# Rows normalised, split and scattered before the expert tiles, halves fetched by a transposing transfer, and a new order of each engine's work

## The chip, the cores and the metric

The kernel runs on one core of a Trainium2 chip. A core has a matrix engine (TensorE, "PE" in the profile, its weight loads "PEld"), VectorE ("DVE"), ScalarE ("ACT"), GpSimd ("POOL") and SyncE ("SP"), which mainly issues transfers. Each engine executes its own stream of instructions in order and waits on semaphores for the others. Sixteen DMA engines carry the transfers. The metric is the device time of one execution in microseconds (us). Three runs of the kernel before took 492.33, 501.55 and 499.98 us, median 499.98.

## The reference

The input `x` is 16 x 256 tokens of 256 features, so T = 4096 rows of D = 256. There are two layers with residuals.

```
x = x + xattn(layernorm(x), ctx, ctx)       # per token: 16 heads of 16 features attend to each other, causal over heads
x = x + ffn(layernorm(x), ...)              # mixture of E = 8 experts, one per token

# ffn:
logits = xf @ gate_w.T + gate_b;  top1 = argmax(logits)
for e in range(8):
    h = relu(xf @ w1[e].T + b1[e])          # 256 -> 1024
    y = h @ w2[e].T + b2[e]                 # 1024 -> 256
    out += where(top1 == e, y, 0)
```

Everything is fp32. To keep that precision the kernel splits fp32 operands into two fp16 halves (a high part and the rest) and adds the products that matter.

## The kernel before, in words

**The attention** goes in 16 steps of 256 tokens (`NC` = 16). A step has a score product of 96 small matmuls (line 1111), a softmax on DVE, ACT and POOL, four transposes of the weights on TensorE (line 1129), and an output product of 96 matmuls (line 1143). The stationary operands of both products are block diagonal. They are built in SBUF by transfers that "spread" a compact tile `qv_hl` into a zeroed part of `arena`: eight small transfers a step, five issued by SP and three by ACT (`spread_part`, line 305; 307 for the last two steps). Step i's spread carries the values of step i and the queries of step i+2, so it waits for output product i-1 and score product i, and output product i waits for it. The fp16 rests of keys, queries and values are made on POOL (lines 995, 987, 1003).

**The groups.** Four steps make a group of 1024 tokens (`NG` = 4). When its outputs are there, TensorE computes gate logits (line 1171) and turns the rows back to token order (line 1156); ACT copies them to `pay` (line 531), DVE takes mean and variance (lines 726 to 735), POOL takes the power -0.5 (line 1029), DVE writes -mean/std beside it (line 738). DVE picks the expert (`choose`) and TensorE ranks the tokens, and POOL scatters the rows of `pay` to `sorted_rows` in DRAM, sorted by expert, with eight indirect transfers (line 1050). A row of `pay` has ROW = 260 words: 256 of x, the shift, the scale, the token number and a zero. After the last group SP fills the gaps behind each expert's rows with twelve transfers (`fill`, line 433).

**The expert tiles.** 39 tiles of 128 sorted rows follow (`NTILES` = 39). Tiles 0 to 8 may start after the second group is scattered, tiles 9 to 16 after the third, tiles 17 to 38 after the fourth. For each tile SP reads its place from a list, fetches its rows (line 451, buffers `FR` = 6) and its expert's biases (lines 456 and 457). ACT normalises the rows (line 566, in `expert_inputs`), TensorE transposes them with two fp32 transposes (line 1196), ACT casts the high half out of PSUM (line 571) and DVE makes the low half (line 906). Then come `ups`, 8 blocks of 6 matmuls (line 1229), into two PSUM banks; DVE adds the bias (line 915), ACT takes the relu as high half (line 580), DVE the rest (line 926); `downs`, 8 blocks of 2 matmuls (lines 1245 and 1246); DVE adds the result to the row (line 940), to which POOL had added the second bias (line 1069), and POOL scatters it to the output (line 1076).

**The order of the work.** On each engine the work is written as several generators ("lanes"), each yielding a due time before each piece. `weave` (line 41) runs, piece by piece, the lane with the earliest due time, and so makes the engine's one stream. The due times are numbers written by hand or by a rule: `tile_at(j)` is 240 + 5.7 j, and blocks of `ups` and `downs` of neighbouring tiles alternate one by one. The due times set only the order: a piece waits in its engine's stream for its semaphores, and everything behind it waits too. The precision of the products, the buffers of hidden units (`h_in`, two halves) and the two PSUM banks of each product are the same for all tiles.

## Time and profile before

| | |
|---|---|
| runs | 492.33, 501.55, 499.98 us, median 499.98 |
| profiled execution | span 492.6 us from the first to the last instruction; no time outside the span is given for it |
| PE, DVE, POOL, ACT busy | 82%, 70%, 42%, 36% of the span |
| mean granted TensorE clock | 0.962 of full speed |
| costliest group | line 1229 on PE, 158.6 us |

The span is 0.3 us over the fastest of the three runs and 7.4 us under their median. The attention's first output product starts at 47.0 us and its last one ends at 238.3. The first expert block on PE starts at 241.1 and the last instruction ends at 492.6. A busy time on PE is the sum of durations of pipelined matmuls, so it must be read beside the starts of the instructions.

### The profile page before, as it was taken

Reading aid. Unit: us, or ns where it says so; the run is one execution under the profiler, and the core shown is the slowest. Engines: PE = TensorE matmul, PEld = TensorE weight load, DVE = VectorE, ACT = ScalarE, POOL = GpSimd, SP = SyncE. Lnnn points to the kernel's source line nnn. Section 1 sums busy time; section 2 is a strip of 40 time slices with the busy share of each in tenths; the row PEclk is TensorE's granted clock in tenths of the full one; section 3 lists DMA queues with packets and bytes.
Section 4 is the critical chain, followed back from the end, with each engine's and each line's share of the span. In section 5 each row is a group of like instructions: output and inputs, shape, how many; then the busy total and the mean of one; then the engine's idle time right before and its main releaser. Section 6 shows DMA issues by size and latency. Waiting matters only on the chain.

```text
span 492.6 us, 16316 instructions
## 1 busy us (share of the span) xinstructions
PE 402.1 (82%) x5967; PEld 338.3 (69%) x5967; DVE 346.3 (70%) x777; ACT 177.5 (36%) x317; POOL 208.7 (42%) x213
## 2 busy tenths in 40 slices
PE   0135868888888866897999999779999999999992
PEld 0025757887787765896887877557778877877871
DVE  7978969789945863477757877457666666766662
ACT  3343255542624221342434433224333333433420
POOL 8345374334673467523723242642333323233221
PEclk9999999999999999975699999889999999999998
DMA  8999578899685664377612232544333322222210
GB/s 282 414 305 218 135 170 241 212 259 260 160 220 119 152 167 107 106 173 181 207 45 67 68 76 81 185 131 155 90 68 77 77 62 62 69 60 61 84 31 0
DMA packets 105162, 69.39 MB, mean 141 GB/s; under 512 B 78077, under 2 KB 88190, under 8 KB 104576
## 3 DMA queue, kind: packets, MB, share of 16 engines
q1 hardware_dynamic: 75696, 56.67, 41.9%
q10 hardware_dynamic: 25984, 3.21, 4.6%
q0 software_dynamic: 3408, 8.46, 4.6%
q8 instruction: 53, 0.87, 0.7%
q14 instruction: 21, 0.17, 0.1%
HBM read 48.28 MB, written 12.57 MB: 124 GB/s over the span
## 4 chain that ended last, share of the span: by engine, by line
PE 55%; DMA 11%; SPq 9%; DVE 9%; issue 6%; POOL 5%; ACT 2%; ACTq 1%; another core or an unknown queue 1%; POOLq 0%; DVEq 0%
PE s_ps L1229 20%; SPq L305 8%; PE at_ps L1245 6%; DMA arena<-qv_hl 6%; PE pv_ps L1245 6%; PE pv_ps L1143 6%; PE s_ps L1111 3%; PE lg_ps L1171 3%; PE pv_ps L1246 3%; PE at_ps L1246 3%; POOL qv_hl L987 2%; PE tr_ps L1156 2%; DMA arena<-x 2%; PE st_ps L1196 2%; POOL k_hl L995 1%
## 5 line engine op out<-in xcount | busy, mean ns | idle before, releaser
L1229 PEld LDWEIGHTS s_ps<-arena 128*128 x1872 | 132.7, 99 | 52.2 <-issue 14.6
L1229 PE MATMUL s_ps<-arena 128*128 128x128 f16 x1872 | 158.6, 222 | 8.4 <-DVE arena L906 5.1
L915 DVE SCALAR_TENSOR_TENSOR arena<-arena,s_ps 128x512 f32<-128x512 f32 x78 | 53.6, 687 | 48.6 <-PE s_ps L1229 35.9
L1076 POOL DMA_INDIRECT result<-arena x39 | 38.8, 995 | 95.5 <-DVE arena L940 91.6
L1111 PEld LDWEIGHTS s_ps<-k_hl,arena 128*128 128x128 f16 x1536 | 54.3, 118 | 29.9 <-DMA arena<-qv_hl 22.1
L1111 PE MATMUL s_ps<-k_hl,arena 128*128 128x16 f16 x1536 | 54.7, 179 | 23.3 <-DMA arena<-qv_hl 19.3
L1143 PE MATMUL pv_ps<-a_hl,arena 128*128 128x16 f16 x1536 | 54.7, 179 | 19.7 <-DMA arena<-qv_hl 15.9
L1143 PEld LDWEIGHTS pv_ps<-a_hl,arena 128*128 128x128 f16 x1536 | 53.5, 118 | 22.8 <-DMA arena<-qv_hl 18.3
L1245 PE MATMUL at_ps<-arena,k_in 128*128 x160 | 60.9, 383 | 0.8 <-DVE k_hl L926 0.6
L1245 PE MATMUL pv_ps<-arena,x_in 128*128 x152 | 58.1, 383 | 0.1
L1069 POOL TENSOR_TENSOR arena<-arena 128x256 f32<-128x256 f32 x39 | 30.7, 786 | 60.7 <-DMA arena<-b 60.6
L580 ACT ACTIVATE k_in<-arena 128x512 f16<-128x512 f32 x40 | 25.2, 630 | 65.7 <-DVE arena L915 60.3
L580 ACT ACTIVATE x_in<-arena 128x512 f16<-128x512 f32 x38 | 23.9, 630 | 69.0 <-DVE arena L915 60.4
L898 DVE SCALAR_TENSOR_TENSOR arena<-arena 128x512 f16<-128x512 f32 x56 | 48.0, 926 | 0.8 <-ACT arena L558 0.7
L1246 PE MATMUL at_ps<-arena,k_hl 128*128 x160 | 43.8, 274 | 0.1
L1246 PE MATMUL pv_ps<-arena,x_in 128*128 x152 | 41.8, 275 | 0.0
L1050 POOL DMA_INDIRECT sorted_rows<-pay,slot_i x32 | 34.2, 1067 | 15.9 <-DVE slot_i L802 8.1
L558 ACT ACTIVATE arena<-arena 128x512 f16<-128x512 f32 x56 | 32.0, 621 | 17.4 <-DMA arena<-w 13.7
L926 DVE SCALAR_TENSOR_TENSOR k_hl<-arena,k_in 128x512 f16<-128x512 f32 x40 | 27.7, 693 | 11.0 <-ACT k_in L580 10.7
L1003 POOL TENSOR_TENSOR qv_hl<-v_in,qv_hl 128x512 f16<-128x512 f32 x16 | 21.6, 1353 | 30.6 <-ACT qv_hl L493 30.6
L926 DVE SCALAR_TENSOR_TENSOR x_in<-arena,x_in 128x512 f16<-128x512 f32 x38 | 26.9, 709 | 8.8 <-ACT x_in L580 8.5
L987 POOL TENSOR_TENSOR qv_hl<-x_in,qv_hl 128x512 f16<-128x512 f32 x16 | 22.1, 1384 | 20.7 <-ACT qv_hl L475 20.7
(143 smaller groups left out, 614.2 us busy)
## 6 DMA issues: line engine op xcount, KB each, us to landing
arena<-w SPq DMA_DIRECT2D x28, 512.0 KB, 6.1
arena<-sorted_rows SPq DMA_DIRECT2D x39, 130.0 KB, 2.4
arena<-b SPq DMA_DIRECT2D x39, 128.0 KB
arena<-qv_hl SPq DMA_DIRECT2D x70, 64.0 KB, 3.5
k_in<-k_t SPq DMA_DIRECT2D x16, 256.0 KB, 3.9
v_in<-v_t SPq DMA_DIRECT2D x16, 256.0 KB
arena<-x SPq DMA_DIRECT2D x4, 1024.0 KB, 12.1
o_sb<-x_r SPq DMA_DIRECT2D x16, 256.0 KB, 3.8
```

The source lines that it names most:

```text
L305: eng.dma_start(to, qv_hl[part, at].rearrange("p s b c u a -> p (s b) c u a")).then_inc(s_bd[i % 2], 16)
L580: eng.activation(h_hi[j % 2][:, c * HALF:(c + 1) * HALF], h_in[:, c], ACT.Relu).then_inc(s_h_hi, 1)
L898: eng.scalar_tensor_tensor(out=lo, in0=src, scalar=W_SCALE, in1=hi, op0=ALU.mult, op1=ALU.subtract).then_inc(s_w_lo, 1)
L915: eng.scalar_tensor_tensor(out=h_in[:, c].rearrange("p (k t) -> p k t", t=P), in0=bias, scalar=W_SCALE, in1=h_ps[c][:].rearrange("p (k t) ...
L926: eng.scalar_tensor_tensor(out=h_lo[j % 2][:, cols], in0=h_in[:, c], scalar=0.0, in1=h_hi[j % 2][:, cols], op0=ALU.max, op1=ALU.subtract). ...
L1050: eng.indirect_dma_start(out=sorted_rows, out_offset=bass.IndirectOffsetOnAxis(ap=slot_i[:, b:b + 1], axis=0), in_=pay[:, b, :], in_offset ...
L1076: eng.indirect_dma_start(out=out, out_offset=bass.IndirectOffsetOnAxis(ap=rows[:, r, :].bitcast(I32)[:, D + 2:D + 3], axis=0), in_=rows[:, ...
L1111: m = eng.matmul(s[:, n], q_bd[i % 2][:, n // 2, :, n % 2, q], k_hl[:, n, k, :], start=False, stop=(n, q) == (BLK - 1, 1))
L1143: m = eng.matmul(o[:, n], v_bd[i][:, n // 2, :, n % 2, v], a_hl[:, n, a, :], start=(n, a, v) == (0, 0, 0), stop=(n, v) == (BLK - 1, 1))
L1229: k = eng.matmul(o, weights_of(j, w + k_ * H + n * P, P), xt[:, j % 2, k_ * P:(k_ + 1) * P], start=k_ == 0 and w is HI_1 and xt is xt_hi, ...
L1245: eng.matmul(y[:], h_hi[j % 2][:, n * P:(n + 1) * P], weights_of(j, at, 2 * D), start=n == 0, stop=False)
L1246: k = eng.matmul(y[:, 0:D], h_lo[j % 2][:, n * P:(n + 1) * P], weights_of(j, at, D), start=False, stop=n == KH - 1)
```

## The change: what it does

1. **Rows are normalised per group.** A new lane `normalised_rows` on ACT computes, for each of 32 blocks of 128 rows, the normalised row into `xn1`, and casts it four blocks at a time to an fp16 high half `x1_hi`. A new lane `low_rows` on POOL subtracts it, four blocks at a time, for the low half `x1_lo`. Both halves stand in `pay` behind the old 260 words, so a row has ROW = 516 words, and the scatters (line 1050 before) and the fills carry the longer rows. The scatters wait for the low halves too.
2. **Tiles fetch the halves transposed.** For each tile SP issues a transposing transfer of 128 rows x 512 fp16 from DRAM into `xt` (three buffers, `XB`), besides the old 260 words into `rows`. Lane `expert_inputs` is gone from ACT, PE and DVE, and so is the PSUM use. The product of the first layer reads `xt` directly.
3. **Waits.** The transfer for tile j waits for `ups` of tile j-3. POOL's residual add waits for the rows themselves, not for ACT's normalising. DVE's bias add of a tile waits for the rest of the tile before it (`s_h_lo`).
4. **A new order.** The due times in the lanes are replaced by a table `TIMES` by engine and lane, which `weave` sorts. In it `ups` come 8 blocks together, in pairs of tiles with 2 blocks of `downs` between the two and 14 behind them. 21 blocks of `ups` (tiles 0, 1 and most of 2) stand ahead of the last output product on PE, and SP has the first fetches (rows of tiles 0, 1 and 2) ahead of the last spread. The first transfers of the program are in another order, and nearly all pieces of the attention change places.
5. `dynamic_dma_scratch_size` is 4096.

The core of the diff:

```diff
-def weave(*lanes):
-    due = [(next(lane, None), n) for n, lane in enumerate(lanes)]
...
+def weave(times, **lanes):
+    turns = sorted((t, n, k) for n, name in enumerate(lanes) for k, t in enumerate(times[name]))
+    lane = list(lanes.values())
+    for steps in lane:
+        next(steps)
+    for _, n, _ in turns:
+        next(lane[n], None)
...
-    ROW = D + 4
+    FETCHED = D + 4
+    ROW = FETCHED + D
+    sorted_halves = sorted_rows.bitcast(F16)
+        xn1 = sb("xn1", [P, G // 2, D])
+        x1_hi, x1_lo = [pay[:, :, FETCHED:].bitcast(F16)[:, :, n * D:(n + 1) * D] for n in range(2)]
-        FR = 6
+        FR, XB = 6, 3
-        TILE = 5.7
+        TILE = 5.3
...
 # SP, fetch
-                    eng.dma_start(rows[:, r, :], sorted_rows[bass.ds(row, P), :]).then_inc(s_rows[r], 16)
-                    yield tile_at(j) - 2.6
+                    if j >= XB:
+                        sp.wait_ge(s_up, 2 * (j - XB + 1))
+                    eng.dma_start_transpose(xt[:, j % XB], sorted_halves[bass.ds(row, P), 2 * FETCHED:]
+                                            ).then_inc(s_xt[j % XB], 16)
+                    eng.dma_start(rows[:, r, :], sorted_rows[bass.ds(row, P), 0:FETCHED]).then_inc(s_rows[r], 16)
+                    yield
...
 # ACT
-            def expert_inputs():
-                for j in range(NTILES):
...
+            def normalised_rows():
+                for g in range(NG):
+                    for m in range(2):
+                        half = slice(m * G // 2, (m + 1) * G // 2)
+                        for b in range(half.start, half.stop):
+                            yield
+                            act.wait_ge(s_ln1, g + 1)
+                            act.wait_ge(s_x1_lo, 2 * g + m)
+                            eng.activation(xn1[:, b - half.start], pay[:, b, 0:D], ACT.Identity, scale=pay[:, b, D + 1:D + 2],
+                                           bias=pay[:, b, D:D + 1]).then_inc(s_xn1, 1)
+                        yield
+                        act.wait_ge(s_xn1, G * g + half.stop)
+                        eng.copy(x1_hi[:, half], xn1[:]).then_inc(s_x1_hi, 1)
...
 # DVE
-            def expert_inputs():
...
 # hiddens
+                        dve.wait_ge(s_h_lo, 2 * (j - 1) + c + 1)
...
 # POOL
+            def low_rows():
+                for g in range(NG):
+                    for m in range(2):
+                        half = slice(m * G // 2, (m + 1) * G // 2)
+                        yield
+                        pool.wait_ge(s_x1_hi, 2 * g + m + 1)
+                        eng.tensor_tensor(x1_lo[:, half], xn1[:], x1_hi[:, half], ALU.subtract).then_inc(s_x1_lo, 1)
 # scatters
+                        pool.wait_ge(s_x1_lo, 2 * g + 2)
 # residuals
-                    pool.wait_ge(s_xn2, j + 1)
+                    pool.wait_ge(s_rows[j % FR], 16 * (j // FR + 1))
...
 # PE
-            def expert_inputs():
-                for j in range(NTILES):
-                    yield tile_at(j) + 0.6
...
-                            pe.wait_ge(s_xt_lo, j + 1)
-                            pe.wait_ge(s_xt_hi, j + 1)
+                            pe.wait_ge(s_xt[j % XB], 16 * (j // XB + 1))
...
-    nc = bacc.Bacc("TRN2", target_bir_lowering=False, num_devices=1)
+    nc = bacc.Bacc("TRN2", target_bir_lowering=False, num_devices=1, dynamic_dma_scratch_size=4096)
```

## Rows read from the trace of the kernel before

**Rows 1.** The page's span and its busy times of PE and DVE.

```profile
span 492.6 us, 16316 instructions
PE 402.1 (82%) x5967; PEld 338.3 (69%) x5967; DVE 346.3 (70%) x777; ACT 177.5 (36%) x317; POOL 208.7 (42%) x213
```

**Rows 2.** Busy time by stage; then mean granted clock, DMA share, GB/s.

```profile
47.00:235.00 188.00, 153.08 (x3063) 140.91 (x3064) 138.25 (x329) 73.77 (x128) 93.20 (x80) 0.95 0.71 178
216.00:243.30 27.30, 23.11 (x473) 21.38 (x471) 21.04 (x59) 10.43 (x18) 14.02 (x13) 0.50 0.67 196
241.00:300.00 59.00, 57.09 (x625) 47.10 (x624) 44.68 (x110) 23.26 (x45) 22.70 (x27) 0.98 0.28 75
300.00:350.00 50.00, 44.49 (x484) 34.44 (x483) 31.03 (x76) 14.97 (x28) 20.18 (x22) 0.93 0.44 140
350.00:478.00 128.00, 126.48 (x1477) 99.76 (x1476) 84.37 (x157) 46.55 (x89) 40.43 (x45) 1.00 0.27 67
```

**Rows 3.** Timeline of PE: starts of tiles 17 and 38, and a transpose pair.

```profile
355.23 0.62 PE L1229 MATMUL s_ps<-arena 128*128 128x128 f16 x6 [0.40 <-issue]
...
358.82 0.50 PE L1229 MATMUL s_ps<-arena 128*128 128x128 f16 x6
359.16 0.39 PE L1196 MATMUL st_ps<-ident,arena 128*128 128x128 f32 x2
359.38 0.38 PE L1245 MATMUL at_ps<-arena,k_in 128*128 x1
...
474.94 0.50 PE L1229 MATMUL s_ps<-arena 128*128 128x128 f16 x6
```

**Rows 4.** The transposes alone: duration in ns (min, median, max), first and last start.

```profile
L1196 PE MATMUL st_ps<-ident,arena x78: 272/278/456, 238.1 to 473.2; 128*128 128x128 f32 x78
```

**Rows 5.** The chain that ended last, within two attention steps: start, us, what.

```profile
110.94 3.39 PE pv_ps L1143 x96
...
114.46 0.60 SPq L305
...
118.19 3.47 DMA arena<-qv_hl
...
121.71 3.38 PE pv_ps L1143 x96
```

**Rows 6.** Timeline of PE: first and last output product, first expert block.

```profile
46.99 3.37 PE L1143 MATMUL pv_ps<-a_hl,arena 128*128 128x16 f16 x96 [2.23 <-DMA arena<-qv_hl]
...
237.83 0.45 PE L1143 MATMUL pv_ps<-a_hl,arena 128*128 128x16 f16 x9 [0.50 <-issue]
...
241.12 2.10 PE L1229 MATMUL s_ps<-arena 128*128 128x128 f16 x18
```

**Rows 7.** A stall at tile 11: ACT, PE; and DVE's group, 300 to 350.

```profile
312.82 0.37 ACT L571 CAST arena<-st_ps 128x256 f16<-128x256 f32 x1 [3.27 <-remote]
314.01 0.34 PE L1229 MATMUL s_ps<-arena 128*128 128x128 f16 x3 [2.66 <-DVE arena L906]
L906 DVE TENSOR_TENSOR arena<-st_ps,arena 128x256 f16<-128x256 f32 x7 | 2.9, 419 | 5.7 <-issue 3.0 <-ACT arena L571 2.8
```

**Rows 8.** Small-piece queue (packets, MB, share of 16 engines); the fetch's landing.

```profile
q10 hardware_dynamic: 25984, 3.21, 4.6%
arena<-sorted_rows SPq DMA_DIRECT2D x39, 130.0 KB, 2.4
```

**Rows 9.** Timeline of SP's queue: one tile's bias loads and the next fetch.

```profile
407.07 0.33 SPq L456 DMA_DIRECT2D arena<-b  x1
407.59 0.33 SPq L457 DMA_DIRECT2D arena<-b  x1
409.00 0.24 SPq L451 DMA_DIRECT2D arena<-sorted_rows  x1
```

**Rows 10.** Groups: ACT normalising (300 to 350), POOL rests and scatters (40 to 235).

```profile
L566 ACT ACTIVATE arena<-arena 128x256 f32<-128x256 f32 x7 | 4.1, 592 | 2.0 <-issue 1.4 <-DMA arena<-sorted_rows 0.6
L995 POOL TENSOR_TENSOR k_hl<-k_in,k_hl 128x512 f16<-128x512 f32 x14 | 17.0, 1215 | 26.4 <-ACT k_hl L484 26.4
L1050 POOL DMA_INDIRECT sorted_rows<-pay,slot_i x16 | 16.4, 1024 | 7.2 <-issue 3.6 <-DVE slot_i L802 3.5
```

More of the change, by code:

```diff
@@ L38, in wait_ge @@
             self.passed[sem] = value
-def weave(*lanes):
-    due = [(next(lane, None), n) for n, lane in enumerate(lanes)]
-    due = [d for d in due if d[0] is not None]
-    while due:
-        turn = min(due)
-        due.remove(turn)
-        again = next(lanes[turn[1]], None)
-        if again is not None:
-            due.append((again, turn[1]))
+def weave(times, **lanes):
[5 more added lines that the diff above has]
+        next(lane[n], None)
+    assert all(next(steps, True) for steps in lane)
 def xattn_moe_kernel(nc, x, x_t, x_r, k_t, v_t, gate_w, gate_b, w1, b1, w2, b2, out):
@@ L210, in xattn_moe_kernel @@
         s_rows = [sem(f"s_rows{n}") for n in range(FR)]
+        s_xt = [sem(f"s_xt{n}") for n in range(XB)]
         s_b1, s_b2 = [[sem(f"{w}_{n}") for n in range(2)] for w in ("s_b1", "s_b2")]
@@ L425, in fill @@
                     for m in range(1 if n < E - 1 else 1 + SPARE // (2 * P)):
-                        yield fill_at(next(at))
+                        yield
                         if n + m == 0:
```

423 lines of the change are left out of this document (236 added, 187 removed), and 98 rows, old and new, of tables (TIMES, act, op1).

## The prediction, as it was put on record before the changed kernel was run

> **What bounds the kernel now.** I read the page first: PE is busy 402.1 of 492.6 us, more than any other engine [rows 1]. Then the busy times by stage [rows 2], which show two kernels in one. In the attention, from 47 to 235 us, PE is busy 153.1 of 188 us and no engine fills the stretch. From 350 to 478 us PE is busy 126.5 of 128 us and DVE 84.4: there the matrix engine is the bound. Between them, from 300 to 350, PE is busy 44.5 of 50. Then the chain that ended last. In the attention it runs round a loop: output product, five issues on SP's queue, the landing of the spread, output product again. One turn is 121.71 - 110.94 = 10.8 us [rows 5]. From the first output product to the end of the last there are 237.83 + 0.45 - 46.99 = 191.3 us [rows 6]; fifteen turns of 10.8 and one product of 3.4 would be 165. So about 26 us of the attention are neither PE work nor the loop, but pieces that stood behind others in an engine's stream. In the expert stage tile 17 starts at 355.23 and tile 38 at 474.94 [rows 3], which is 119.7 / 21 = 5.70 us a tile.
>
> **The change part by part.** The sum is made against the profiled execution, whose span is 492.6 us. That is 0.3 over the fastest run and 7.4 under the median of 499.98.
>
> *a. The transposes leave PE.* There are 78, two a tile, with a median duration of 278 ns [rows 4]. Multiplied out that is 21.7 us, and it is the wrong reading, because durations on PE overlap. The pair starts at 359.16 and the next matmul at 359.38 [rows 3]: the pair costs PE 0.22 us. So 39 x 0.22 = 8.6 us go, and the pitch falls from 5.70 to 5.48 us. The Trainium skill ("TensorE: Matmul & The Clock Gate", Part 4: PE-mode transpose) gives about 275 ns for one in a kernel's context and says that access latency is most of it; the duration here agrees, and a sum made with it would be 78 x 0.275 = 21.5 us by that page, where the starts in the trace show a pair at 0.22. The other instructions that go (two on ACT and one on DVE a tile) free engines that have time to spare in that stage [rows 2]; I cost them at nothing, and PE is their cover.
>
> *b. New work in the groups.* ACT gets 32 normalisings at 0.59 us [rows 10] and 8 casts of 1024 columns. POOL gets 8 subtractions of 1024 columns, twice the 512 of line 995 at 1.2 us [rows 10], so 2.4 us each. In the attention ACT is busy 73.8 and POOL 93.2 of 188 us [rows 2]. Three groups bring POOL 6 x 2.4 = 14 us. POOL makes the rests of queries and values that a spread waits for, so a subtraction in front of one delays a turn of the loop. This can cost from 0 to 14 us; it is taken within the next term. The longer scatters and fills carry about twice the bytes. The DMA share is 0.44 where the fills are [rows 2], and in the new order all fills stand before the fetch of tile 11, so tile 17 does not wait for them: nothing.
>
> *c. The new order in the attention.* It can give back at most the 26 us above. It can give nothing, or cost, say, one more turn, 11 us, since each engine is in order and a piece that is late holds all behind it. I take half of the most, 13 us gained, because group work (gates, turned rows, rests) has to go somewhere in each four steps and PE has 35 idle us there, not more.
>
> *d. Expert work ahead of the last output product.* Before, the first expert block starts at 241.12, 2.8 us after the last output product [rows 6]. Now 21 blocks of 6 matmuls stand ahead of it. A block takes 0.34 us (358.82 to 359.16, rows 3), so 21 x 0.34 = 7 us go into PE's idle time. Bounds 0 to 7, I take 7.
>
> *e. The stalls near the fourth group.* Tile 11 starts after 2.66 us of idle PE, released by line 906, which had waited for line 571, which had waited 3.27 us [rows 7]; these two lines no longer exist. PE's idle time from 300 to 350 is 5.5 us, and two stretches at half clock of 3.4 us follow the stalls. I take 5 us gained, between 0 (another wait takes their place) and 10. What is late next: in SP's stream tile 10's fetch is between the fills, which wait for the fourth group's count, so a late routing would starve PE there.
>
> *f. SP's queue.* Per tile it takes 409.00 + 0.24 - 407.07 = 2.2 us of 5.70 [rows 9], and one issue more is 0.24 to 0.9 us (line 305's issues, rows 5, are 0.6 and up). Steadily this is hidden. But three fetches now stand ahead of the last spread, which the last output product waits for. That can cost 1 to 7 us; I take 2.
>
> *g. The clock.* From 216 to 243 the granted clock was 0.50, that is 1.2 GHz in place of 2.4, and it came when little wide work was there to be slowed [rows 2]. With expert blocks in that stretch such a spell would cost up to 13 us (half of 27). I take 2, since it may not come at all.
>
> The transposing transfer itself has no row. It moves 128 KB a tile. From below, the plain fetch of 130 KB lands in 2.4 us [rows 8]. From above, as pieces of 32 bytes: the queue of small pieces took 4.6% of 16 x 492.6 us for 25984 packets, 14 ns each [rows 8], and 4096 pieces over 16 engines are 3.6 us, or 7.2 if reading and writing do not overlap. I take 3.6 us plus 2.4 for landing, 6 us. The window from the end of `ups` j-3 to `ups` j is two tiles, about 11 us. So it is hidden and costs nothing. The Trainium skill ("VectorE: DVE Perf Modes", The three transpose paths) gives 1309 ns for a 128 x 128 two-byte transpose by DMA; four of them would be 5.2 us a tile, an estimate by that page, just inside the pitch, so the sum by it would not change but the margin is thin.
>
> Sum: 492.6 - 8.6 - 13 - 7 - 5 + 2 + 2 = 463.0 us. The runs before lie from 0.3 under to 9 over their profile, so I add 4, about half of the 7.4 to the median: **467 us**.
>
> **The rivals.**
>
> *Attention unmoved.* The new order brings new late pieces for old ones (c is 0) and the early blocks stand waiting in PE's stream (d is 0). Left are a, e, f: 492.6 - 8.6 - 5 + 2 = 481, with 4 added 485. For it: PE's and DVE's streams are already dense, and POOL has 14 us more. Against it: 26 us are there to be had.
>
> *Everything given back.* Also e stays, and the late routing at tile 10 costs what the transposes gave: about 495. This is also the case in which the change does not do what it says.
>
> *The transposing transfer is the bound (slower).* Its place is the fetch of every tile from tile 3 on. If the pieces are read and written one after the other, 7.2 us a transfer, and one transfer goes at a time, the pitch is 7.2 in place of 5.48: 36 x 1.7 = 62 us on top of 467, so 529 us. It decides from 5.48 us a transfer, or from a landing later than 11 us; at 6.3 us the gain is used up. For it: the pieces on the SBUF side are short, and such a stream has no row. Against it: DMA share is 0.27 in that stage [rows 2].
>
> **How the numbers follow.** Forecast 0.66, with a range of its own from 452 to 484 (c from 24 to 0, g up to 10). Attention unmoved 0.15 (478 to 494). Given back 0.06. The transfer as the bound 0.13. The range from 450 to 500 leaves out the last and a little below. A measurement of this kernel tells about 2% from no change, here 490 to 510. Faster by over 2%: 0.66 + 0.11 of the second case, 0.77. Within 2%: 0.04 + 0.06 = 0.10. Slower 0.13.
>
> **What the profile after would show.** a: no line like 1196, and tiles 5.4 to 5.5 us apart near the end; if they are 5.2, the pair was worth its duration. b: POOL subtractions near 2.4 us. c: the last output product ends near 225 to 230 us. d: expert blocks before it. e: no idle PE of about 3 us between tiles 10 and 14. f: landing of the transposing transfer well under 11 us. The prediction is wrong if `ups` of late tiles wait for `xt`, or if the output products still come 12.5 us apart on the mean.

## The result, and the profile of the changed kernel

The changed kernel took 530.42 us (median of 4 runs, 529.35 to 532.71) beside 500.69 us for the kernel before (492.33 to 501.55): the ratio is 1.074, with a 95% interval from 1.067 to 1.080. It is slower by 7.4%, where 467 us, with a range from 450 to 500, had been forecast: the prediction was wrong.

The page, in answer to [rows 1]. Columns as there.

```profile
span 529.3 us, 16204 instructions
PE 422.1 (80%) x5889; PEld 348.7 (66%) x5889; DVE 341.3 (64%) x738; ACT 165.1 (31%) x279; POOL 231.7 (44%) x221
```

TensorE has 5889 matmuls in place of 5967: exactly the 78 transposes are gone. Yet it is busy 20 us more. So the busy times of the matmuls that were there before must be longer, by clock or by their order; the stages tell which.

The stages, in answer to [rows 2], and the stretch at half clock: window, length, busy time of PE, PEld, DVE, ACT, POOL, granted clock, DMA share, GB/s.

```profile
47.00:235.00 188.00, 141.02 (x2789) 130.86 (x2790) 137.16 (x265) 82.93 (x143) 97.61 (x82) 0.84 0.71 179
235.00:300.00 65.00, 55.06 (x737) 47.74 (x735) 41.35 (x109) 20.11 (x35) 27.26 (x27) 0.79 0.56 142
300.00:350.00 50.00, 43.43 (x398) 29.96 (x397) 32.25 (x83) 14.20 (x24) 26.05 (x23) 0.93 0.88 242
350.00:478.00 128.00, 125.32 (x1321) 97.11 (x1319) 66.90 (x122) 25.49 (x42) 39.49 (x41) 1.00 0.38 81
173.80:259.20 85.40, 62.74 (x1212) 58.46 (x1213) 60.52 (x152) 36.25 (x62) 43.85 (x37) 0.50 0.67 164
```

Two things stand out. From 47 to 235 us TensorE issues 2789 matmuls, not 3063: the attention is behind. From 350 to 478 us it is busy 125.3 of 128 us at full clock, as before, but with 1321 matmuls in place of 1477. The transposes of some 23 tiles are 46 of the 156 missing; the rest are matmuls that follow each other more slowly.

TensorE's timeline, in answer to [rows 3, 6]: first output product (L1313), first expert block (L1386), last output product, first of the fourth group's turned outputs (L1325), starts of tiles 18 and 38.

```profile
53.13 3.34 PE L1313 MATMUL pv_ps<-a_hl,arena 128*128 128x16 f16 x96 [6.24 <-DVE a_hl L886]
...
253.38 8.28 PE L1386 MATMUL s_ps<-arena 128*128 128x128 f16 x96 [3.68 <-issue]
...
264.53 3.34 PE L1313 MATMUL pv_ps<-a_hl,arena 128*128 128x16 f16 x96
...
273.38 0.69 PE L1325 MATMUL tr_ps<-ident,o_sb 128*128 128x128 f32 x4
...
389.54 3.58 PE L1386 MATMUL s_ps<-arena 128*128 128x128 f16 x48
393.02 0.38 PE L1402 MATMUL at_ps<-arena,k_in 128*128 x1
...
514.44 1.70 PE L1386 MATMUL s_ps<-arena 128*128 128x128 f16 x24
```

From the starts the 36.7 us of span divide into stages. They are read in the same way in every kernel below: the end of the last output product, the start of tile 17, the start of tile 38.

| | last product ends | tile 17 | tile 38 | span |
|---|---|---|---|---|
| before | 238.3 | 355.2 | 474.9 | 492.6 |
| changed | 267.9 | 381.1 | 514.4 | 529.3 |
| longer by stage | +29.6 | -3.7 | +13.6 | -2.8 |

The attention loses 29.6 us and the steady expert stage 13.6 (about 2 us of this come back in the last column: tiles now go in pairs, and tile 17 is the second of its pair, tile 38 the first of its own). The steady pitch is (514.44 - 389.54) / 20 = 6.2 us, where 5.48 was forecast. The row of tile 18 says where: its 48 up matmuls (L1386) stand in a row and take 393.02 - 389.54 = 3.48 us, 72 ns each. In the kernel before 6 of them take 0.34 us [rows 3], 57 ns each.

VectorE's timeline, in two places that TensorE waited for:

```profile
45.06 7.32 DVE L1069 SCALAR_TENSOR_TENSOR arena<-arena 128x512 f16<-128x512 f32 x6
52.31 0.68 DVE L886 TENSOR_TENSOR a_hl<-at_ps,a_hl 128x512 f16<-128x512 f32 x1
...
114.44 0.69 DVE L868 TENSOR_REDUCE rowmax<-s_ps 128x32 f32<-128x512 f32 x1 [2.28 <-PE s_ps L1283]
...
117.84 2.38 DVE L903 BATCH_NORM_STATS2 bn<-pay 128x6 f32<-128x256 f32 x7
120.14 0.62 DVE L907 BATCH_NORM_AGGREGATE bn<-bn 128x2 f32<-128x6 f32 x8
...
123.26 0.69 DVE L875 TENSOR_TENSOR a_sb<-s_ps,rowmax 128x512 f32<-128x512 f32 x1
```

Six low halves of expert weights (7.3 us) stand ahead of the first softmax result. Later a whole group's layer norm stands between the row maximum (L868) at 114.44 and the subtraction (L875) at 123.26.

SP's queue ahead of the last output product: the third fetch (a transposing transfer), then the last spread.

```profile
254.79 1.22 SPq L646 DMA_TRANSPOSE arena<-sorted_rows  x1
256.21 0.41 SPq L648 DMA_DIRECT2D arena<-sorted_rows  x1
256.68 3.78 SPq L506 DMA_DIRECT2D arena<-qv_hl  x5
```

### The profile page after: what moved, and what is told of

The parts are those of the page before. It is cut to its first block, busy times and chain, and to the rows that moved or that the text cites. A ratio compares the mean times of both kernels' runs of the same rounds, so it can differ in the third digit from the quotient of the medians.

```text
span 529.3 us, 16204 instructions
## 1 busy us (share of the span) xinstructions
PE 422.1 (80%) x5889; PEld 348.7 (66%) x5889; DVE 341.3 (64%) x738; ACT 165.1 (31%) x279; POOL 231.7 (44%) x221
## 4 chain that ended last, share of the span: by engine, by line
PE 66%; DVE 20%; issue 6%; POOL 3%; DMA 2%; SPq 1%; ACT 1%; POOLq 0%; DVEq 0%; ACTq 0%
PE s_ps L1386 26%; PE at_ps L1402 7%; PE pv_ps L1402 6%; PE pv_ps L1313 6%; PE lg_ps L1339 5%; PE s_ps L1283 5%; DVE arena L1069 4%; PE at_ps L1403 3%; PE pv_ps L1403 3%; PE tr_ps L1325 2%; DVE bn L903 2%; PE at_ps L1300 2%; DVE xbn L823 1%; DMA arena<-x 1%; POOL xstat L1146 1%
## 5 line engine op out<-in xcount | busy, mean ns | idle before, releaser
L1386 PE MATMUL s_ps<-arena 128*128 128x128 f16 x1872 | 144.2, 220 | 10.4 <-issue 8.7
L1386 PEld LDWEIGHTS s_ps<-arena 128*128 x1872 | 127.9, 98 | 30.2 <-issue 15.0
L1246 POOL DMA_INDIRECT result<-arena x39 | 46.3, 1187 | 79.9 <-DVE arena L1105 71.6
L1313 PE MATMUL pv_ps<-a_hl,arena 128*128 128x16 f16 x1536 | 54.6, 180 | 30.1 <-DVE a_hl L886 20.6
L1313 PEld LDWEIGHTS pv_ps<-a_hl,arena 128*128 128x128 f16 x1536 | 54.0, 118 | 33.9 <-issue 19.7
L769 ACT ACTIVATE k_in<-arena 128x512 f16<-128x512 f32 x40 | 23.3, 623 | 156.5 <-PE at_ps L1403 135.7
L1105 DVE SCALAR_TENSOR_TENSOR arena<-at_ps,arena 128x256 f32<-128x256 f32 x40 | 17.0, 424 | 79.0 <-PE at_ps L1403 78.4
L1402 PE MATMUL at_ps<-arena,k_in 128*128 x160 | 56.9, 390 | 2.1 <-DVE k_hl L1091 1.7
L1402 PE MATMUL pv_ps<-arena,x_in 128*128 x152 | 51.5, 384 | 1.9 <-DVE x_in L1091 1.9
L1403 PE MATMUL pv_ps<-arena,x_in 128*128 x152 | 41.9, 275 | 0.0
L1175 POOL TENSOR_TENSOR a_sb<-a_sb,inverse 128x512 f32<-128x512 f32 x16 | 18.4, 1150 | 34.8 <-DVE inverse L883 34.8
L1300 PE MATMUL at_ps<-ident,a_sb 128*128 128x128 f32 x64 | 17.7, 429 | 16.4 <-POOL a_sb L1175 16.0
L1339 PEld LDWEIGHTS lg_ps<-gate_bd,o_sb 128*128 128x128 f32 x128 | 28.8, 312 | 2.0 <-issue 1.6
```

The lines of the kernel that those rows point to most:

```text
L769: eng.activation(h_hi[j % 2][:, c * HALF:(c + 1) * HALF], h_in[:, c], ACT.Relu).then_inc(s_h_hi, 1)
L1246: eng.indirect_dma_start(out=out, out_offset=bass.IndirectOffsetOnAxis(ap=rows[:, r, :].bitcast(I32)[:, D + 2:D + 3], axis=0), in_=rows[:, ...
L1313: m = eng.matmul(o[:, n], v_bd[i][:, n // 2, :, n % 2, v], a_hl[:, n, a, :], start=(n, a, v) == (0, 0, 0), stop=(n, v) == (BLK - 1, 1))
L1339: m = eng.matmul(LG, o_sb[:, :, h], gate_bd[:, h].rearrange("p b e -> p (b e)"), start=h == 0, stop=h == HEADS - 1)
L1386: k = eng.matmul(o, weights_of(j, w + k_ * H + n * P, P), xt[:, j % XB, a + k_], start=(k_, w, a) == (0, HI_1, 0), stop=k_ == KD - 1 and w ...
L1402: eng.matmul(y[:], h_hi[j % 2][:, n * P:(n + 1) * P], weights_of(j, at, 2 * D), start=n == 0, stop=False)
```

## The experiments

Chips differ, for the kernel before most of all: 476 to 487 us on three of them, 492 to 505 on the others. So each ratio is to the kernel before on the same chip, and stages are compared by their starts. "Old order" is that of the kernel before, "new order" that of the changed kernel; an order is edited by renumbering the tables of positions. Every kernel with the changed data path also has its smaller parts (VectorE's wait for the rests of the tile before, the scratch size of 4096); no run separates these.

**The yardstick: the changed kernel again.**

> The changed kernel, unaltered, on the same chip as the others of this call, as the yardstick for them. Expected: last output product ends near 268 us, pitch 6.2 us, 1.06 to 1.08 times the kernel before.

Measured: 523.60 us, ratio 1.086 [1.079, 1.094]; last product ends at 265.6, tile 17 at 372.7, tile 38 at 506.3, span 521.1. As expected. Its clock was 0.997 on the mean in place of 0.909. Of the 8.2 us between the two spans, 2.3 lie in the attention (267.9 - 265.6) and 6.1 between there and tile 17, after the long stretch at half clock had ended at 259.2. The clock is not shown to be the cause. The four runs of the first result took 529.35, 529.84, 531.01 and 532.71 us with mean granted clocks of 0.854, 0.910, 0.909 and 0.983, so the shortest had the lowest clock; of the four runs here the shortest had the highest (522.88 us with 0.997, 524.80 with 0.865). Neither way is it more than 3.4 us. The other difference between the two is the chip.

**The changed data path in the old order (e1).** The new pieces are slotted in behind their group's mean and variance:

```diff
 # positions on GpSimd, shortened
-scatters of a group: 8 pieces, one by one between the attention's
+low_rows 0, low_rows 1 of the group, then its 8 scatters
 # on ScalarE: 10 normalised_rows behind the group's layer_norms
 # expert stage: up and down blocks alternate one by one, as before
```

> The changed data path (normalised rows as halves, transposing transfer, no transposes on TensorE) with every lane back in the order of the kernel before; the new pieces (normalising on ScalarE, subtraction on GpSimd) stand one group step behind their group's mean and variance. Theory 1, the new order is the cost and the data path a gain: last output product ends near 238 to 242, tile pitch 5.48 us (5.70 less the 0.22 of a pair of transposes), time about 480 to 487 us. Rival, the data path (transposing transfer, its time on SP's queue, longer rows) is the cost: pitch stays at 6.2 or the attention still ends near 268, time 515 to 530 us.

Measured: 503.46 us, ratio 1.048 [1.041, 1.056]; last product ends at 254.5, tiles 17 and 38 at 374.5 and 486.8, so 5.35 us a tile, span 500.9. On another chip 502.48 and 1.050. Both theories hit one half: the pitch is what the transposes should give, but the attention is 16.2 us longer than before (254.5 - 238.3) though its order is the old one. The longest of the waits is this, in TensorE's timeline:

```profile
211.21 1.11 PE L1242 MATMUL at_ps<-ident,a_sb 128*128 128x128 f32 x4 [9.96 <-POOL a_sb L1117]
```

and GpSimd's timeline ahead of it:

```profile
196.35 2.16 POOL L1142 TENSOR_TENSOR pay<-xn,pay 128x1024 f16<-128x1024 f32 x1
203.41 2.12 POOL L1142 TENSOR_TENSOR pay<-xn,pay 128x1024 f16<-128x1024 f32 x1 [4.90 <-ACT pay L702]
206.43 1.07 POOL L1162 DMA_INDIRECT sorted_rows<-pay,slot_i  x1 [0.90 <-POOL pay L1142]
207.81 0.98 POOL L1162 DMA_INDIRECT sorted_rows<-pay,slot_i  x1 [0.30 <-issue]
209.09 0.97 POOL L1162 DMA_INDIRECT sorted_rows<-pay,slot_i  x1 [0.30 <-issue]
210.08 1.07 POOL L1117 TENSOR_TENSOR a_sb<-a_sb,inverse 128x512 f32<-128x512 f32 x1
```

GpSimd is idle 4.90 us in front of the second subtraction, waiting for ScalarE's cast (L702), then issues three scatters, and only then scales the softmax weights (L1117) for which TensorE has been idle almost 10 us. The granted clock is no rival here: the kernel before ends its attention at 236.6 with a clock of 0.81 in it (its second profile, below), this kernel at 253.2 with 0.80 (its second profile, too).

**Alternating blocks in the new order (e2).**

```diff
 # TensorE from tile 17 on
-ups j (8 blocks in a row), downs (8 blocks in a row)
+ups j block 0, downs block, ups j block 1, downs block, ...
 # VectorE and GpSimd, same tiles: rests, results and stores in the order that this needs
```

> The changed kernel with its new order up to tile 16, and from tile 17 on the blocks of up and down products alternate again, one by one, as in the kernel before. Theory, 48 up matmuls in a row are slower than the same ones between down products: pitch falls from 6.2 to 5.48 us over 22 tiles, so 16 us less, time about 514 us; the attention stays as it is (last output product ends near 268). Rival, the pitch is set by the transposing transfer or by VectorE: pitch and time unchanged, 529 to 531 us.

Measured: 502.62 us, ratio 1.048 [1.040, 1.057]; last product ends at 266.8, tile 17 at 375.8, tile 38 at 486.7: (486.7 - 375.8) / 21 = 5.28 us a tile. Against the ratio 1.086 of the unaltered changed kernel this one edit gives back 0.038 of 482, 18 us. (The medians, on two chips with nearly the same kernel before, differ by 21.) Transfer, work and instructions are the same; only the order from tile 17 on differs.

**The same from the other side: the kernel before with blocks in a row (e3).**

```diff
-yield tile_at(j) + 2.6 + UNIT * n
+yield tile_at(j) + 2.6 + 0.01 * n
...
-yield tile_at(j) + 8.65 + UNIT * n
+yield tile_at(j) + 8.65 + 0.01 * n
```

> The kernel before, with its transposes on TensorE, where only the order of the expert stage is changed: the eight up blocks of a tile stand in a row, and the eight down blocks too. Theory as for the alternating kernel, from the other side: pitch rises from 5.70 to about 6.4 us, over 39 tiles 28 us more, time about 520 us. Rival, the order of blocks costs nothing: pitch 5.70, time 493 to 500 us.

Measured: 576.59 us, ratio 1.198 [1.188, 1.207]; pitch 8.22 us. The direction holds, the size was far under. Its timeline on TensorE, tile after tile:

```profile
393.05 3.88 PE L1229 MATMUL s_ps<-arena 128*128 128x128 f16 x48 [1.23 <-DVE arena L906]
401.14 3.97 PE L1229 MATMUL s_ps<-arena 128*128 128x128 f16 x48 [1.23 <-DVE arena L906]
405.11 0.38 PE L1245 MATMUL at_ps<-arena,k_in 128*128 x1
```

The 48 take 3.97 us (83 ns each), and TensorE waits another 1.23 us for the turned rows' rest (L906): with the blocks in a row nothing is left to cover the chain transposes, ScalarE, VectorE. Of the 1.8 us by which 8.2 is over the 6.4 that I expected, this wait is 1.2; the rest is mostly that the row is slower here than in the changed kernel, 83 ns a matmul and not 72.

**Weights at a fixed address (e4).** The kernel leaves out the choice of the expert: every tile multiplies by the first one's weights.

```diff
-weights_at[j] = nc.snap(shared[n, m] // E ** (slot % SHARED) % E * (2 * SLOT), ...)
+weights_at[j] = 0
...
-return weight_bytes[:, 2 * at:][:, bass.ds(weights_at[j], 2 * cols)].bitcast(F16)
+return weight_bytes[:, 2 * at:2 * at + 2 * cols].bitcast(F16)
```

Measured: 499.26 us, ratio 1.042 [1.032, 1.051]. Its timeline on TensorE, with the blocks still in rows:

```profile
470.81 2.84 PE L1385 MATMUL s_ps<-arena 128*128 128x128 f16 x48
473.49 0.38 PE L1401 MATMUL at_ps<-arena,k_in 128*128 128x512 f16 x1
...
474.14 2.06 PE L1385 MATMUL s_ps<-arena 128*128 128x128 f16 x34
```

The 48 take 473.49 - 470.81 = 2.68 us, 56 ns each; two tiles take 10.6 us where nothing else is late (5.68 a tile on the mean from tile 17 to 38, with single gaps). How a row gets slow can be counted. Up matmuls in equal windows of 0.6 us, in the row of tile 18 of the changed kernel (from its second window on), then in the row of e4 above (window, length, busy time and count of PE and of PEld, granted clock, DMA share, GB/s; a matmul that touches two windows counts in both):

```profile
390.14:390.74 0.60, 0.60 (x14) 0.59 (x12) 1.00 0.00 0
390.74:391.34 0.60, 0.60 (x12) 0.55 (x9) 1.00 0.12 7
391.34:391.94 0.60, 0.60 (x8) 0.43 (x7) 1.00 0.24 77
391.94:392.54 0.60, 0.60 (x9) 0.55 (x9) 1.00 0.24 82
...
471.41:472.01 0.60, 0.60 (x15) 0.60 (x12) 1.00 0.35 106
472.01:472.61 0.60, 0.60 (x15) 0.60 (x13) 1.00 0.24 68
```

The rows cost time ahead of tile 17 too, which e2 left as it was. From the last output product to tile 17 e4 takes 97.9 us where the second profile of the changed kernel takes 107.1.

**New pieces later in the old order (e5).**

```diff
 # distance behind the group's mean and variance, us (groups 1, 2, 3)
-low_rows 0: 4, 4, 4    low_rows 1: 8, 8, 8     scatters: from 8.3
+low_rows 0: 16, 5, 6   low_rows 1: 32, 9.5, 11  scatters: 1 to 2 apart
```

What this changes in GpSimd's stream is less than the text below says. The first group's subtractions go behind several other pieces, and its scatters are spread. For the second group only the softmax weights of output product 12 move, from behind the third scatter to between the two subtractions. The third group's order stays.

> The changed data path in the order of the kernel before, as in the first experiment, but the normalising of a group's rows and the two subtractions on GpSimd stand 4 to 9 us later in their engines' streams for the second and third group, up to 32 us later for the first. In the first experiment GpSimd stood 4.9 us before line 1142 of that kernel and the softmax weights behind it were late, so output products 12 and 13 came 13 us later than in the kernel before. Theory, the price of the group's new work is such waits at the head of an in-order queue: the last output product ends at 241 to 247 in place of 254.5, time 488 to 496. Rival, the work itself (17 us on GpSimd, 27 us on ScalarE) is the price wherever it stands: 252 or later, time unchanged at 500 to 505.

Measured: 505.07 us, ratio 1.047 [1.039, 1.054]; last product ends at 255.2. My theory missed the end, though it held on the way: output product 8 began 3.2 us earlier than in e1 (152.7) and product 12 6.9 us earlier (208.6), but products 13 to 15 0.7 to 3 us later. GpSimd's and TensorE's timelines between products 12 and 13 show where the gain went:

```profile
206.78 2.13 POOL L1142 TENSOR_TENSOR pay<-xn,pay 128x1024 f16<-128x1024 f32 x1 [3.54 <-ACT pay L702]
...
222.60 1.07 POOL L1117 TENSOR_TENSOR a_sb<-a_sb,inverse 128x512 f32<-128x512 f32 x1
223.73 1.12 PE L1242 MATMUL at_ps<-ident,a_sb 128*128 128x128 f32 x4 [9.88 <-POOL a_sb L1117]
```

Between the two GpSimd rows stand the group's eight scatters, about 1 us each and 0.3 apart, and two rests. The weights of product 12 got past them, so those of product 13 wait: the price moved by one product.

**The last output product ahead of the expert work (e6).**

```diff
 # SP's queue
-fetch 0, fetch 1, fetch 2, spread 15
+spread 15, fetch 0, fetch 1, fetch 2
 # TensorE
-21 up blocks, output product 15
+output product 15, 21 up blocks
```

> The changed kernel with one move: the last spread on SP's queue stands ahead of the first fetch, and the last output product ahead of the 21 up blocks on TensorE. Theory, these 21 blocks and three fetches delay the last product by some 11 us (its weights were ready at 252.6, it began at 264.5): it now ends at 256 to 257, the fourth group's gates come 8 to 11 us earlier, time 4 to 10 us less than the changed kernel on this chip. Rival, the early blocks are a gain as forecast (they fill idle time): the time rises by up to 7 us or stays.

Measured: 525.79 us, ratio 1.092 [1.084, 1.100]. Its yardstick is the 523.60 us of the changed kernel on the same chip. The product ends at 254.2 in place of 265.6, as expected. The time does not follow: tile 17 starts at 375.1 (372.7). The timeline on TensorE:

```profile
254.79 8.22 PE L1328 MATMUL s_ps<-arena 128*128 128x128 f16 x96 [0.58 <-issue]
263.52 4.01 PE L1328 MATMUL s_ps<-arena 128*128 128x128 f16 x48 [0.51 <-DVE arena L1022]
269.81 4.70 PE L1328 MATMUL s_ps<-arena 128*128 128x128 f16 x48 [2.28 <-DVE arena L1022]
274.35 0.67 PE L1267 MATMUL tr_ps<-ident,o_sb 128*128 128x128 f32 x4
```

The fourth group's first transposes stand behind four tiles' up blocks and come at 274.35, no earlier than without the move (270.8). So the early blocks are worth about 2 us where 7 were forecast (525.79 - 523.60; the two intervals overlap, the single runs, 522.88 to 524.80 and 525.22 to 528.43, do not), and the 11.4 us by which they and the fetches delay the last product are nearly free.

**Three local moves (e7).** The first is that of e6; the other two:

```diff
 # VectorE, start
-weights 9 to 14, softmax 4
+softmax 4, weights 9 to 14
 # VectorE and ScalarE, first group
-layer_norms 0 to 17, softmax 31, ..., softmax 32, 33
+softmax 31, layer_norms 0 to 7, softmax 32, 33, layer_norms 8 to 17
-normalised_rows 0, keys 8, exponentials 12
+exponentials 12, normalised_rows 0, keys 8
```

> The changed kernel with three moves. One is that of the last output product. Second, six low halves of expert weights on VectorE stand behind the first softmax product in place of ahead of it. Third, for the first group the softmax step of output product 6 stands ahead of the layer norm on VectorE and ahead of the first normalising on ScalarE. Theory, the new order loses its time where such a lump stands ahead of a piece that TensorE waits for: output product 0 begins at 47 to 48 in place of 53.1, product 6 at 121 to 124 in place of 135, and most of this is kept to the end (last product ends at 242 to 250), time 15 to 25 us less than the changed kernel. Rival, other pieces are late as well and the time is given back at once: product 0 and 6 earlier, but the last product still ends at 255 or later.

Measured: 530.52 us, ratio 1.100 [1.093, 1.108], so 4.7 us more than e6. Output product 0 begins at 49.3 (53.1), product 1 at 63 as before, product 6 at 138.6 (134.4); the last one ends at 257.7 (254.2 in e6). VectorE's timeline in place of the lump:

```profile
117.81 2.37 DVE L845 BATCH_NORM_STATS2 bn<-pay 128x6 f32<-128x256 f32 x7
123.38 0.69 DVE L822 TENSOR_REDUCE inverse<-a_sb 128x32 f32<-128x512 f32 x1 [3.19 <-ACT a_sb L674]
```

The subtraction comes 7 us earlier (116.29), but now VectorE stands idle 3.19 us for ScalarE, with the rest of the layer norm behind it. Moving the lumps that I had read as the cause gained nothing; each move made a new wait.

**Thin group work (e8 in the old order, e9 in the new, e12 all groups).**

```diff
+w = D if g == 0 else 8        # e12: w = 8 for all
-eng.activation(xn1[:, b - half.start], pay[:, b, 0:D], ...)
+eng.activation(xn1[:, b - half.start, 0:w], pay[:, b, 0:w], ...)
-eng.tensor_tensor(x1_lo[:, half], xn1[:], x1_hi[:, half], ALU.subtract)
+eng.tensor_tensor(x1_lo[:, half, 0:w], xn1[:, :, 0:w], x1_hi[:, half, 0:w], ALU.subtract)
```

These kernels leave out most of the normalising: 8 of 256 columns of a row are worked, the others are stale or zero.

> The first experiment (changed data path, old order), but from the second group on the normalisings, casts and subtractions of the group work only 8 of 256 columns of each row; instructions, order and waits stay, the first group is worked in full, and most of the later groups' halves are stale. Theory, the work on ScalarE and GpSimd (8 x 0.52 + 2 x 1.05 us and 2 x 2.15 us a group) is what makes the attention longer: up to output product 7 nothing changes, and the last product ends at 242 to 246 in place of 254.5, time about 492 to 496. Rival, the waits and the longer hold of the group's buffer are the price (its scatters now wait for normalised rows): the last product still ends at 251 to 255, time 500 to 505.

Measured: 495.49 us, ratio 0.993 [0.988, 0.997] on a chip where the kernel before takes 497; last product ends at 247.3. So 7.2 of the 16 us in the attention go with the later groups' work (254.5 - 247.3), the theory, and about 9 stay, the rival.

> The changed kernel in its own order with the same thinning from the second group on (8 of 256 columns; most of the later groups' halves are stale). Theory, the new order is late for its own reasons: product 8 still begins near 161, the last product ends at 258 to 263 in place of 265.6, time 517 to 522. Rival, the new order is slow because of the group work: last product at 250 or earlier, time 508 to 512.

Measured: 525.38 us, ratio 1.049 [1.040, 1.058]; last product ends at 261.4. The theory holds for the attention (265.6 - 261.4 = 4.2 us); the time lies between those of the changed kernel on its two chips (523.60 and 530.42), which was not run on this one.

> As the thinned kernel in the old order, but the first group's normalising, casts and subtractions also work 8 of 256 columns (the halves are zeros set at the start). Theory, the first group's work costs the attention about 7 us as the second and third group's did together: output product 8 begins at 150 to 152 in place of 156, the last product ends at 240 to 243 in place of 247.3 (238.3 in the kernel before), so nearly the whole 16 us of the changed data path in the attention is this work. Rival, half of it is waits that stay: product 8 still at 155 to 156, the last product at 246 or later.

Measured: 489.77 us, ratio 1.021 [1.012, 1.030] on a chip where the kernel before takes 479; last product ends at 245.8, product 8 begins at 153.5. The rival holds: of the 15 us by which e1 on this chip is behind (253.2 - 238.3, or 16.6 by the 236.6 of the second profile of the kernel before), the work is 7.4 and the rest stays with hardly any work. The waits of TensorE from 120 to 250 us show what stays: first e12, then the kernel before (us in total, times, longest).

```profile
PE at_ps L1245 <- POOL a_sb L1119: 10.2, 5, 6.4
```

```profile
PE at_ps L1129 <- POOL a_sb L1012: 2.1, 2, 1.2
```

GpSimd's scaled weights are late by 8 us more. The longest of these waits, on GpSimd and TensorE:

```profile
200.18 0.24 POOL L1145 TENSOR_TENSOR pay<-xn,pay 128x32 f16<-128x32 f32 x1 [7.28 <-ACT pay L703]
...
204.95 1.08 POOL L1119 TENSOR_TENSOR a_sb<-a_sb,inverse 128x512 f32<-128x512 f32 x1
206.08 1.12 PE L1245 MATMUL at_ps<-ident,a_sb 128*128 128x128 f32 x4 [6.40 <-POOL a_sb L1119]
```

The subtraction takes only 0.24 us now, but GpSimd still stands idle 7.28 us in front of it for ScalarE's cast, which comes late in ScalarE's own stream. Then come three of the group's scatters, which need the whole group's halves and so stand behind the subtraction, and only then the weights. The larger part is the wait of one engine for another, the smaller the scatters.

**A plain transfer in place of the transposing one (e10).**

```diff
-eng.dma_start_transpose(xt[:, j % XB], sorted_halves[bass.ds(row, P), 2 * FETCHED:])
+eng.dma_start(xt[:, j % XB].rearrange("p n t -> p (n t)"), sorted_halves[bass.ds(row, P), 2 * FETCHED:])
```

> The first experiment with a plain transfer of the same 128 KB in place of the transposing one, so TensorE multiplies by rows that are not turned. Theory, the transposing transfer is hidden: pitch stays 5.3, time within 3 us of 503; what may change is the start of the first tiles, which wait for a landing. Rival, it costs where a fetch is urgent (tiles 0 to 3, and behind the fourth group): 5 us or more less.

Measured: 499.76 us, ratio 1.015 [1.011, 1.020] on the chip with 497; last product ends at 255.0, tile 17 at 371.7, tile 38 at 482.9 (5.29 a tile), span 497.0. The kernel leaves out the turning: TensorE multiplies by rows as they are. The span is 3.9 us under e1's on other chips, most of it between the last product and tile 17 (116.7 against 120.0). e1 was not run on this chip, but e8 was, with the transposing transfer, and has 120.4 there. In this stage TensorE waits for fetched rows 3.8 us in e1 and 6.6 us in e8, and here not at all. So the rival has a small part of the truth: among the fills the transposing transfer is not quite hidden, and costs 3 to 4 us. The pitch does not need it to be faster. The pages' issues say how long the two take, the changed kernel again first (queue, kind, count, median us to landing):

```profile
arena<-sorted_rows SPq DMA_TRANSPOSE x39, 3.7
```

```profile
arena<-sorted_rows SPq DMA_DIRECT2D x39, 128.0 KB, 2.4
```

**The best parts joined (e11).**

```diff
 # up to the first expert block: old order; to tile 16: new order
 # from tile 17 on: blocks alternate
```

> The changed data path, put together from the best parts seen so far: up to the first expert block every lane in the order of the kernel before, from there to tile 16 in the order of the changed kernel, from tile 17 on up and down blocks alternating. Theory, the stages add: last output product near 255 us, 109 us from there to tile 17 (as in the changed kernel), pitch 5.3, span 488 to 492, so 1 to 3% more than the kernel before on a chip where that takes 482, level with it where it takes 498. Rival, the middle stage of the changed order depends on its own attention order: 500 or more.

> The first experiment again, on the chip of this call, as the yardstick for the other two: last output product ends near 254.5 us, span about 501.

Measured: 505.99 us for the joined kernel, ratio 1.058 [1.052, 1.065], and 502.48 for e1 on the same chip, ratio 1.050 [1.044, 1.056]. The last product ended at 269.9, since the early blocks stood ahead of it again, and the 109 us from there to tile 17 that I had counted on were no gain by themselves: they leave out the early blocks (107.1 with these ahead of the last product, 120.9 without, in e6). Stages cut at one event don't add when work is moved across that event. No version here that does the whole work beats the kernel before.

**The kernel before again.**

> The kernel before, unaltered, for a second profile. The runs of it beside the experiments took 476 to 487 us on three chips and 492 to 504 on another, where its first profile shows 492.3. Expected: the last output product ends at 234 to 238, pitch 5.5 in place of 5.70, span 478 to 500 with the chip; if the pitch is 5.5, the changed kernel's transposes were worth 5.5 - 5.3 = 0.2 us a tile, as its own forecast term says.

Measured: 497.47 us, on a chip of the slower kind. Span 495.0; last product ends at 236.6; tiles 17 to 38 from 352.7 to 477.2, 5.93 us a tile. Undisturbed tiles are 5.5 apart; the slow ones (up to 6.4) have TensorE idle at the tile's edge, at full clock:

```profile
471.28 0.69 PE L1229 MATMUL s_ps<-arena 128*128 128x128 f16 x6 [0.49 <-issue]
```

The kernels with the changed data path and alternating blocks have 5.28 to 5.37 on every chip. I have no profile of the kernel before on a chip where it takes 480, so whether these edges make the difference between chips stays open.

## Why the prediction was wrong, step by step

The sum gave a span of 463.0 us; it is 529.3. Put on the stages, the forecast terms had the last product at 229.3 (238.3 - 13 + 2 + 2), then 101.2 us to tile 17 (116.9 - 7 - 5 and the transposes of 17 tiles) and 115.1 to tile 38. So the miss of 66 us is 39 in the attention, 12 behind it and 18 in the steady stage, less 3 at the end. Three terms failed: the price of a block in a row (a, d), the new work put at nothing (b), and the gain from the order (c).

**a. Transposes: right; blocks in a row: the first failure.** Forecast 0.22 us a tile. Undisturbed tiles went from 5.5 to 5.28 (e2). The count by starts, not the durations, was the right reading. On the mean the pitch fell by more, from 5.70 to 5.28, since the gaps at the edges of tiles, which the forecast had left in, went too. The Trainium skill ("TensorE: Matmul & The Clock Gate", Part 4: PE-mode transpose) gives about 275 ns for one, which as a term of the sum would be 0.55 us a tile, an estimate by that page; the trace shows less than half of that. But the forecast pitch 5.48 assumed that the blocks still alternate. The diff's table of positions shows eight up blocks in a row, and I had counted them at 0.34 us each, a duration taken between down products. There the price does not hold: the blocks in a row cost 72 ns a matmul in place of 57, the pitch became 6.2, and e2 gives 18 us back with that edit alone, from tile 17 on. e4 shows that the register addressing is what the rows stumble over, and that the tiles ahead of 17 pay for it too, about 9 us.

**b. New work in the groups: the second failure.** The subtractions took the time forecast (2.15 us where I had said 2.4). But I took the price "within the next term", that is, as hidden in a forecast gain. Alone, in the old order, the data path costs the attention 15 to 16 us: 7.4 the work, the rest waits that stay when the work is thinned away, of GpSimd for ScalarE's halves and of the softmax weights behind the scatters (e8, e12; e5 moved them and won nothing). The bound of 14 us that stood in the text was close to what came, but in part by luck: it counted GpSimd's work in front of the rests of queries and values, and what TensorE waited for most was the scaled softmax weights, and about half of the price stayed when the work was nearly gone. It was written as a bound and then given no place of its own in the sum; that was the mistake.

**c. The new order in the attention: no gain, the third failure.** The last product was forecast at 225 to 230 us and came at 267.9. Of the 29.6 us lost, 16 are the data path (e1), 11.4 are expert blocks and fetches ahead of the last product (e6), and 2.3 are the difference between the two profiles of the changed kernel. So with this data path the order itself neither gave nor took: 254.2 in e6, 254.5 in e1. What it would do without the data path was not run, and the 16 need not be the same in both orders: thinning gave 7.2 us in the old one (e8) and 4.2 in the new (e9). The output products begin (264.53 - 53.13) / 15 = 14.1 us apart on the mean, over the 12.5 named as the mark of a wrong forecast. I had seen 26 us of slack and taken half, without a row that said which piece would come earlier. The lumps at 45 and 114 us are real waits, but in e7 moving them gained nothing; which move would is open.

**d. Expert work ahead: about 2 us, not 7.** I had counted PE's idle time ahead of the last product, and not that the fourth group's transposes stand behind the same blocks (273.38 in place of 248.8).

**e. Stalls near the fourth group: partly gone.** From the last product to tile 17 it took 113.2 us in place of 116.9, and 107.1 in the second profile; but this stage leaves out the blocks done early, so it is no clean gain. In e1, where none are early, the stage is 120.0. The waits for line 906 (5.1 us there in the kernel before) are gone, and others took their place: TensorE waits 3.5 us for ScalarE's copy to `pay`, 3.8 for a transposing fetch issued among the fills, and 3.3 with nothing shown. The DMA share from 300 to 350 us went from 0.44 to 0.88 with the longer fills, which the sum had put at nothing; what they cost was not separated.

**f. SP's queue: over the bounds.** The last spread was issued at 256.68 behind three fetches, 255.62 in the second profile, and at 243.75 on the same chip in e6, where it stands ahead of them: 12 us later, with a bound of 7 and 2 taken. The last product came only 11.4 us later and stood behind the early blocks as well; e6 moved both at once, so the two are not told apart, and the whole time moved by 2 us, the other way. A landing of the transposing transfer took 3.7 us, not 6.

**g. The clock.** Half clock came for 85 us, not 27, and the runs show no clear price for it: among the changed kernel's runs on one chip the one with the lowest mean clock is 3.4 us shorter than the one with the highest (0.854 and 0.983), on the other 1.9 us longer (0.865 and 0.997). I had 2, with a bound of 13.

**The rivals.** "The transfer is the bound" gave 529 us, nearly the time measured, and it is false: its mark was a pitch of 7.2 with `ups` waiting for `xt`; the pitch is 6.2 with TensorE busy 125.3 of 128 us, and e2 reaches 5.28 with the same transfer. A right number from a wrong mechanism. "Given back" at 495 was the right kind of case, with a price far too small: nothing in it let the change cost more than it had gained.

## What to carry to other kernels

- A new order of the same instructions can change their durations. Where weights are addressed by a register, count a matmul's price in the neighbourhood where it will stand, not where it stands now: here 57 ns between wide matmuls and 72 to 83 ns in a row.
- Work moved from a bound engine to an idle one isn't free if that engine's stream holds pieces others wait for. Ask what stands behind it, what it waits for itself, and what must now wait for it (here GpSimd waits for ScalarE's halves, the scatters for both, and the softmax weights stand behind all three). Give the bound a place of its own in the sum.
- Slack is a gain only when a row names the piece that comes earlier.

## What the runs showed of the hardware

- A row of 48 matmuls of 128 columns whose weights are addressed by a register takes 3.5 us (tile 18 of the changed kernel) to 4.0 us (e3) in place of 2.68 with fixed addresses (e4). It begins at nearly full pace and slows down within the row; with two wide matmuls after every six it keeps 57 ns (e2).
- The transposing transfer of a 128 x 512 two-byte tile is issued in 1.23 us (median on SP's queue) and lands in 3.7 us, where the plain one lands in 2.4. The Trainium skill ("VectorE: DVE Perf Modes", The three transpose paths) gives 1309 ns for a quarter of it, which makes 5.2 us for four in turn, an estimate by that page; the trace is below that.
- The same program takes 476 to 487 us on some chips and 492 to 505 on others, while the changed one differs by under 2% (523.60 and 530.42 us).
- Up to the end of the attention TensorE runs at half clock for 75 us or more in all but three of the profiles here (27 us in the first of the kernel before, none in the second of the changed kernel and in e7), and the time does not follow it clearly: e1 took 502.85 us in the run with a mean granted clock of 0.833 and 504.17 in the one with 0.987, the changed kernel 524.80 with 0.865 and 522.88 with 0.997.
